# One core, attention beside an expert layer: who copies the expert result out of its bank, and how the first operands come in

## The chip, the cores and the metric

The kernel runs on one core of one Trainium2 chip. The metric is the device time of one execution in microseconds (us); lower is better. A core has five engines that run their own instruction lists and wait for each other by semaphores: TensorE (PE: matmuls, PEld: its weight loads), VectorE (DVE), ScalarE (ACT), GpSimd (POOL) and SyncE (SP), which here only issues transfers. Transfers are carried by 16 DMA engines.

## The reference

For each of 8 batches of 512 tokens with 128 features the kernel computes x + attention(xn) + experts(xn), where xn is x after a layer norm without scale.

```python
qkv = xn @ w_in.T + b_in                      # 16 heads of 8
scores = einsum('bhqd,bhkd->bhqk', q * scale, k) + causal_bias
out = (softmax(scores) @ v) @ w_out.T + b_out
# experts: 8 routed of width 176, the best 2 of each token, and a shared one of width 352
combine = top2(softmax(xn @ gate_w.T)), normalised, * 2.5
y = sum_e combine[:, e] * ((silu(xn @ w_gate[e]) * (xn @ w_up[e])) @ w_down[e])
result = x + out + y + shared_expert(xn)
```

All of it is in float32; the kernel keeps that precision by splitting numbers into parts: the attention's q and k into three bfloat16 parts, the experts' activations and weights into a high and a low part.

## The kernel before

**Stages.** The program of every engine alternates between two stages. In `experts_and_maxima(b, ...)` TensorE runs the gate, up and down matmuls of the 14 expert tiles of batch b, summing the result turned (features by tokens) in the bank `bank_y`; between the tiles it computes the plain scores of batch b in 18 units (`scores`, line 613), of which VectorE takes the row maxima (line 1273). In `attend(i, ...)` TensorE computes the scores of batch i once more, transposed, in 18 units (`scores_t`, line 678, with the mask at 691), into two pairs of banks in turn; ScalarE takes the exponential of each unit (line 974); TensorE weighs v with them (`weigh_v`, line 707). Unit n of `scores_t` waits until ScalarE is done with unit n - 2. The order is written out by hand in each engine's list, and an engine never overtakes within its own.

**What else stands in `attend`.** The front of the next batch is prepared there: ScalarE takes k (line 887), VectorE takes v, splits k, takes q (line 1170), splits q (lines 1160 to 1166), and then adds the tokens to the expert result (`add_tokens`, line 1326), computes the router's weights and more. SyncE writes the parts of k and q to memory (lines 394 and 400) and, once all six writes have landed and half of the transposed units are done, loads them back spread over the partitions as `q_op` and `k_op` (`operands_in`, line 455): 512 KB each for a half of the heads. Behind them stand the routing weights: one small write (line 406) and 18 loads of `cb` (line 411), for GpSimd, which weighs the routed hidden values (line 1055). TensorE starts the plain scores of the next batch (line 613, unit 0) near the end of `attend`; unit 9 is the first to need the second half of the heads.

**The expert result.** In `attend`, ScalarE copies `bank_y` to `yT` (`take_y`, line 958; the profile calls that memory o_sb) behind its second exponential. TensorE turns it back with four transposes (`transpose_y`, line 662) behind unit 3 of the transposed scores, and VectorE adds the tokens to it.

**The first batch** has lists of its own. VectorE normalises, makes `bq_scaled` (line 1500, it needs the q and k weights' semaphore), the low parts of the shared weights (line 1477), splits x, takes the router's maxima and logits (1194, 1196) and v, computes the router's weights (1216 to 1230), casts three constants to bfloat16 (1470 to 1472), copies `combT` (1237), takes q, splits q and k, and only then multiplies the first hidden tile (line 1249). ScalarE converts the weights' high parts (994), takes the turned x, takes the exponential for the router (892), takes k. SyncE issues the token loads of batches 2 to 7 (`tokens_in`, line 366, three of 512 KB) ahead of the first operands.

## Time and profile before

| what | value |
|---|---|
| median of 3 runs | 555.38 us (553.04 to 557.18) |
| the profiled execution | 554.11 us, of which 552.3 us are the span from first to last instruction |
| mean granted clock of TensorE | 0.994 of full speed |
| busy: TensorE, VectorE, ScalarE, GpSimd | 512.5, 430.5, 330.6, 229.6 us |
| one batch in the middle, from one first q projection to the next | 64.0 to 64.8 us |

The profile is read in this order: the busy shares say which engine can bound the kernel; the chain of waits says through which lines the end was reached; the timeline of one stage says which engine waits for which there. A row of the timeline has the start, the length, the engine, the line, the operation with what it writes and reads, how many such instructions were merged, and in brackets the idle time of that engine before it with what ended it. Matmuls overlap, so the lengths of neighbouring TensorE rows can add up to more than the time between them.

### The profile page before, as it was taken

What the parts mean: (1) busy time and instruction counts of PE and PEld (TensorE: products, weight loads), DVE (VectorE), ACT (ScalarE), POOL (GpSimd) and SP (SyncE); (2) the same over time, 40 slices, a digit from 0 to 9 for tenths busy, and PEclk for the clock granted to TensorE, in tenths of its full rate; (3) what the DMA queues carried; (4) which work ended last, traced back from release to release, by engine and by line L of the source; (5) the groups of instructions that cost most, each with busy time, mean ns of one, the idle gap of its engine ahead of it and who ended that gap; (6) DMA issues with size and microseconds to landing.
All of it is one profiled execution on the core that took longest, in us unless ns stands there. A gap on an engine that the chain in (4) does not pass through costs nothing.

```text
span 552.3 us, 16880 instructions
## 1 busy us (share of the span) xinstructions
PE 512.5 (93%) x6840; PEld 321.2 (58%) x6840; DVE 430.5 (78%) x845; ACT 330.6 (60%) x454; POOL 229.6 (42%) x201
## 2 busy tenths in 40 slices
PE   1589999999999999999999999999999999999995
PEld 1355654676557664576546664576646765467643
DVE  3989988899859968598757968599686978489713
ACT  6322489445873469544894458834696348844593
POOL 2026810587007840379005870078403790058600
PEclk9979999999999999999999999999999999999999
DMA  9887016900367005750169003770068302590000
GB/s 261 219 242 181 2 67 163 259 5 11 117 188 196 2 11 162 207 132 1 68 170 258 16 11 116 192 193 1 11 188 219 94 1 78 149 270 16 11 21 21
DMA packets 46896, 62.55 MB, mean 113 GB/s; under 512 B 6672, under 2 KB 30448, under 8 KB 46832
## 3 DMA queue, kind: packets, MB, share of 16 engines
q1 hardware_dynamic: 44124, 58.34, 38.6%
q10 hardware_dynamic: 2708, 3.24, 1.8%
q8 instruction: 54, 0.88, 0.7%
q14 instruction: 10, 0.08, 0.1%
HBM read 45.18 MB, written 15.34 MB: 110 GB/s over the span
## 4 chain that ended last, share of the span: by engine, by line
PE 70%; DVE 8%; ACT 7%; issue 5%; DMA 5%; POOL 4%; SPq 1%; ACTq 0%; DVEq 0%
PE banks L577 9%; PE banks L579 8%; PE banks L578 8%; PE banks L613 7%; PE banks L593 7%; PE banks L707 7%; ACT probs L974 5%; PE banks L678 5%; PE banks L594 4%; PE banks L595 4%; DVE neg_max L1273 3%; DMA k_op<-k_dram 2%; POOL hid_lo L1063 2%; PE banks L532 2%; DMA wqk_sb<-in_wqkT 1%
## 5 line engine op out<-in xcount | busy, mean ns | idle before, releaser
L1273 DVE TENSOR_REDUCE neg_max<-banks 128x2 f32<-128x1024 f32 (+7 forms) x240 | 177.9, 790 | 30.1 <-PE banks L604 28.8
L1063 POOL TENSOR_TENSOR hid_lo<-probs,hid_hi 128x512 fp32r<-128x512 f32 x85 | 109.5, 1288 | 214.5 <-ACT hid_hi L911 214.2
L974 ACT ACTIVATE probs<-banks 128x1024 f32<-128x1024 f32 x144 | 139.1, 1026 | 16.4 <-PE banks L691 15.2
L1055 POOL TENSOR_TENSOR probs<-probs,cb 128x512 f32<-128x512 f32 x88 | 113.1, 1285 | 76.1 <-ACT probs L904 75.5
L904 ACT ACTIVATE probs<-banks 128x512 f32<-128x512 f32 (+1 forms) x112 | 66.8, 598 | 124.2 <-PE banks L579 123.1
L1249 DVE TENSOR_TENSOR probs<-probs,banks 128x512 f32<-128x512 f32 (+1 forms) x112 | 75.9, 679 | 33.3 <-POOL probs L1055 24.9
L577 PE MATMUL banks<-x_hi,w_hi 128*128 128x512 f32 (+1 forms) x224 | 95.6, 427 | 4.8 <-DVE probs L1249 4.1
L579 PE MATMUL banks<-x_hi,w_lo 128*128 128x512 f32 (+1 forms) x224 | 89.5, 400 | 0.0
L578 PE MATMUL banks<-x_lo,w_hi 128*128 128x512 f32 (+1 forms) x224 | 88.9, 397 | 0.0
L911 ACT ACTIVATE hid_hi<-probs 128x512 fp32r<-128x512 f32 (+1 forms) x96 | 60.3, 628 | 38.4 <-DVE probs L1249 38.4
L707 PE MATMUL banks<-probs,v_op 64*32 64x512 f32 (+7 forms) x2048 | 78.5, 410 | 0.0
L678 PE MATMUL banks<-q_op,k_op 64*64 64x512 bf16 (+7 forms) x1024 | 57.4, 295 | 7.2 <-ACT probs L974 6.4
L613 PE MATMUL banks<-k_op,q_op 64*64 64x448 bf16 (+7 forms) x1024 | 54.6, 293 | 5.7 <-DVE neg_max L1273 2.9
L593 PE MATMUL banks<-hid_hi,wd_hi 128*128 128x512 f32 (+1 forms) x112 | 55.3, 494 | 2.6 <-POOL hid_lo L1063 2.3
L577 PEld LDWEIGHTS banks<-x_hi,w_hi 128*128 128x128 f32 (+1 forms) x224 | 42.2, 188 | 21.1 <-DVE probs L1249 5.0
L678 PEld LDWEIGHTS banks<-q_op,k_op 64*64 64x64 bf16 x1024 | 20.2, 105 | 49.4 <-ACT probs L974 31.9
L579 PEld LDWEIGHTS banks<-x_hi,w_lo 128*128 128x128 f32 (+1 forms) x224 | 42.1, 188 | 10.6
L578 PEld LDWEIGHTS banks<-x_lo,w_hi 128*128 128x128 f32 (+1 forms) x224 | 42.4, 189 | 8.5 <-issue 0.5
L707 PEld LDWEIGHTS banks<-probs,v_op 64*32 64x32 f32 x2048 | 30.6, 106 | 27.0 <-issue 16.9
L613 PEld LDWEIGHTS banks<-k_op,q_op 64*64 64x64 bf16 x1024 | 20.6, 105 | 42.6 <-issue 22.4
L594 PE MATMUL banks<-hid_hi,wd_lo 128*128 128x512 f32 (+1 forms) x112 | 44.6, 399 | 0.0
L595 PE MATMUL banks<-hid_lo,wd_hi 128*128 128x512 f32 (+1 forms) x112 | 44.5, 397 | 0.0
(138 smaller groups left out, 556.7 us busy)
## 6 DMA issues: line engine op xcount, KB each, us to landing
cb<-c_dram SPq DMA_DIRECT2D x31, 256.0 KB, 4.0
q_op<-q_dram SPq DMA_DIRECT2D x15, 512.0 KB, 6.3
k_op<-k_dram SPq DMA_DIRECT2D x15, 512.0 KB, 7.4
cb<-c_dram SPq DMA_DIRECT2D x16, 224.0 KB, 4.7
q_dram<-q_parts SPq DMA_DIRECT2D x8, 384.0 KB, 2.9
k_dram<-k_parts SPq DMA_DIRECT2D x8, 384.0 KB, 2.6
cb<-c_dram SPq DMA_DIRECT2D x16, 192.0 KB, 3.8
cb<-c_dram SPq DMA_DIRECT2D x15, 160.0 KB, 4.0
```

The source lines that it names most:

```text
L577: pe.matmul(bank, w_hi[:, w, cols], x_hi[:, :], start=True, stop=False)
L578: pe.matmul(bank, w_hi[:, w, cols], x_lo[:, :], start=False, stop=False)
L579: pe.matmul(bank, w_lo[:, w, cols], x_hi[:, :], start=False, stop=True).then_inc(ready, 1)
L593: pe.matmul(bank_y[:, :], wd_hi[0:n, tile, :], hi, start=(k == 0), stop=False)
L613: pe.matmul(bank[rows, a, at:at + n], q_op[own, 2 * g + c, HALF * jq:HALF * (jq + 1)], k_op[own, 2 * g + c, 0:n], start=first, stop=False, ...
L678: pe.matmul(ring[half(c), 2 * ((n + 1) % 2) + a, at:at + S - HALF * jk], k_op[half(a), 2 * g + c, HALF * jk:HALF * (jk + 1)], q_op[half(a) ...
L707: mm = pe.matmul(nat[32 * j:32 * j + 32, c, HALF * jk:S], v_op[half(c), jk ^ c, t, j, :], probs[half(c), 2 * home_of(units[x]) + a, at[x]: ...
L974: nc.scalar.activation(probs[:, 2 * home_of(n):2 * home_of(n) + 2, :], ring[:, at:at + 2, :], ACT.Exp).then_inc(exp_done, 1)
L1055: nc.gpsimd.tensor_tensor(sg[k % 3][:, :], sg[k % 3][:, :], cb[:, tiles_of(b)[k], :], ALU.mult).then_inc(weighted, 1)
L1063: nc.gpsimd.tensor_tensor(hid_lo[0:n, k % 3, :], hid[k % 3][0:n, :], hid_hi[0:n, k % 3, :].bitcast(F32), ALU.subtract).then_inc(hid_lo_don ...
L1249: nc.vector.tensor_tensor(hid[k % 3][0:n, :], sg[k % 3][0:n, :], ring[0:n, up_bank(k), :], ALU.mult).then_inc(hid_done, 1)
L1273: return nc.vector.tensor_reduce(out, in_, AX.X, ALU.max, negate=True)
```

## The change

Three things are changed.

1. `take_y` moves from ScalarE (behind its second exponential) to VectorE (between taking q and splitting q), and TensorE's `transpose_y` moves from behind unit 3 to behind unit 5 of the transposed scores.
2. In every later batch the first half of the operands is loaded in two quarters: q and k of the first quarter of the heads (256 KB each, counted by `ops_first`), then q and k of the second quarter (`ops_loaded[0]`). Plain scores unit 0 waits for the first pair alone, unit 4 for the second. The first batch was loaded so already.
3. In the first batch the three casts of constants and the taking of q move from VectorE to ScalarE; `bq_scaled` moves behind the router's logits; the three token loads move behind the loads of the routing weights.

On TensorE, in `attend`, before (from unit 3 on; each unit is rows of `q_op,k_op` and a row of masks; `ident_sb,o_sb` is `transpose_y`, `probs,v_op` a weighing):

```order
L678 MATMUL banks<-q_op,k_op 64x448 x4
L678 MATMUL banks<-q_op,k_op 64x64 x4
L691 MATMUL banks<-ident_half,mask_half 64x2x64 x4
L662 MATMUL banks<-ident_sb,o_sb 128x128 x4
L678 MATMUL banks<-q_op,k_op 64x384 x4
L678 MATMUL banks<-q_op,k_op 64x128 x4
L691 MATMUL banks<-ident_half,mask_half 64x2x64 x4
L707 MATMUL banks<-probs,v_op 32x512 x8
L678 MATMUL banks<-q_op,k_op 64x384 x4
L678 MATMUL banks<-q_op,k_op 64x128 x4
L691 MATMUL banks<-ident_half,mask_half 64x2x64 x4
```

and now:

```order
L679 MATMUL banks<-q_op,k_op 64x448 x4
L679 MATMUL banks<-q_op,k_op 64x64 x4
L692 MATMUL banks<-ident_half,mask_half 64x2x64 x4
L679 MATMUL banks<-q_op,k_op 64x384 x4
L679 MATMUL banks<-q_op,k_op 64x128 x4
L692 MATMUL banks<-ident_half,mask_half 64x2x64 x4
L708 MATMUL banks<-probs,v_op 32x512 x8
L679 MATMUL banks<-q_op,k_op 64x384 x4
L679 MATMUL banks<-q_op,k_op 64x128 x4
L692 MATMUL banks<-ident_half,mask_half 64x2x64 x4
L663 MATMUL banks<-ident_sb,o_sb 128x128 x4
L679 MATMUL banks<-q_op,k_op 64x320 x4
L679 MATMUL banks<-q_op,k_op 64x192 x4
```

The four transposes have moved behind the first weighing and unit 5.

On VectorE, at the same place now (`o_sb<-banks` is the copy of `bank_y`):

```order
L1173 TENSOR_SCALAR qk_f<-banks,bq_scaled 128x512
L1178 COPY o_sb<-banks 128x512
L1163 CAST q_parts<-qk_f 128x512
L1165 TENSOR_TENSOR qk_rest<-qk_f,q_parts 128x512
L1167 CAST q_parts<-qk_rest 128x512
L1169 TENSOR_TENSOR q_parts<-qk_rest,q_parts 128x512
L1333 TENSOR_TENSOR x_sb<-banks,x_sb 128x512
```

Before, the same rows stood there without the copy: it lies ahead of the whole split of q.

At the start of the kernel, on ScalarE now (from the second conversion of weights on):

```order
L989 ACTIVATE w_hi<-probs 128x1408
L1004 ACTIVATE ident_bf<-ident_sb 128x128
L1005 ACTIVATE ident_half<-probs 128x64
L1006 ACTIVATE mask_half<-probs 128x64
L893 ACTIVATE rt<-rt 128x32
L1010 ACTIVATE qk_f<-banks,bq_scaled 128x512
L888 ACTIVATE qk_f<-banks,bqk 128x512
L905 ACT_TABLE_LOAD
L905 ACTIVATE probs<-banks 128x512 x2
```

Before, only the rows of `rt<-rt` and of k (`qk_f<-banks,bqk`) stood between the conversion and the table load: the casts now stand ahead of the router's exponential, and q ahead of k.

The diff:

```diff
--- before.py
+++ after.py
@@ -256,6 +256,7 @@
         slots_set = sem("slots_set")
         slots_written = sem("slots_written")
         const_made = sem("const_made")
+        casts_made = sem("casts_made")
         wd_loaded = [sem(f"wd_loaded{n}") for n in range(2)]
         w_hi_done = sem("w_hi_done")
         shared_lo = sem("shared_lo")
@@ -383,10 +384,6 @@
             for dst, src in ((mask_f[0:HALF, :], causal[0:HALF, 0:HALF]), (mask_f[HALF:P, :], causal[0:HALF, 0:HALF]),
                              (ident_f[0:HALF, :], ident[0:HALF, 0:HALF]), (ident_f[HALF:P, :], ident[0:HALF, 0:HALF])):
                 sp.dma_start(dst, src).then_inc(consts_loaded, 16)
-            tokens_in(1)
-            tokens_in(2)
-            tokens_in(3)
-
 
             def k_parts_out(j):
                 sp.wait_ge(ksplit_step, 4 * j + 4)
@@ -450,11 +447,12 @@
 
                     sp.wait_ge(st_ready, ST_ALL * i + ST_ALL * (n + 1) // 2)
                 apart(sp, sp_passed)
-                own = slice(n * PAIRS // 2, (n + 1) * PAIRS // 2)
-                for op, dram in ((q_op, q_dram), (k_op, k_dram)):
-                    sp.dma_start(op[:, own, :].rearrange("p i n -> p (i n)"),
-                                 dram[:, :, :, own, :].rearrange("t s d i n -> (s d) t (i n)")
-                                 ).then_inc(ops_loaded[n], 16)
+                parts = [(slice(0, PAIRS // 4), ops_first), (slice(PAIRS // 4, PAIRS // 2), ops_loaded[0])]
+                for own, loaded in (parts if n == 0 else [(slice(PAIRS // 2, PAIRS), ops_loaded[1])]):
+                    for op, dram in ((q_op, q_dram), (k_op, k_dram)):
+                        sp.dma_start(op[:, own, :].rearrange("p i n -> p (i n)"),
+                                     dram[:, :, :, own, :].rearrange("t s d i n -> (s d) t (i n)")
+                                     ).then_inc(loaded, 16)
 
             def store(i):
                 sp.wait_ge(summed, i + 1)
@@ -488,6 +486,8 @@
             weights_around(1)
             operands_in(0, None, 1)
             weights_around(2)
+            for n in range(1, 4):
+                tokens_in(n)
             sp.dma_start(bo_bc[:, :], b_o.partition_broadcast(P)).then_inc(out_weights, 16)
             for j in range(4):
                 for c in range(2):
@@ -623,11 +623,12 @@
                     pe.wait_ge(ops_first, OP_LOADS * 16)
                 elif i is None and n == OWN_UNITS:
                     pe.wait_ge(ops_loaded[0], OP_LOADS * 16)
-                elif n in (0, NAT_ALL // 2):
-
+                elif n == 0:
+                    pe.wait_ge(ops_first, OP_LOADS * 16 * b + OP_LOADS * 16)
+                elif n in (OWN_UNITS, NAT_ALL // 2):
                     pe.wait_ge(ops_loaded[n // (NAT_ALL // 2)], OP_LOADS * 16 * b + OP_LOADS * 16)
                 if i is None and n == 0:
-                    pe.wait_ge(const_made, 4)
+                    pe.wait_ge(casts_made, 3)
                     pe.wait_ge(q_done, 1)
                     pe.wait_ge(k_done, 1)
                 elif i is None and n == 1:
@@ -830,7 +831,7 @@
                     scores_t(i, n)
                     if n == 2 and front:
                         project_q(i + 1)
-                    if n == 3:
+                    if n == 5:
                         transpose_y(i)
                     if n == TURN_COMB_AT and front:
                         transpose_comb(i + 1)
@@ -953,10 +954,6 @@
                     if 1 <= k < NT - LATE_HIGH:
                         high_hidden(b, k - 1)
 
-            def take_y(i):
-                act.wait_ge(down_done, NT * i + NT)
-                nc.scalar.activation(yT[:, :], bank_y[:, :], ACT.Copy).then_inc(y_taken, 1)
-
             def attend(i, front):
                 if front:
                     take_k(i + 1)
@@ -973,8 +970,6 @@
                     at = 2 * ((n + 1) % 2)
                     nc.scalar.activation(probs[:, 2 * home_of(n):2 * home_of(n) + 2, :], ring[:, at:at + 2, :], ACT.Exp
                                          ).then_inc(exp_done, 1)
-                    if n == 1:
-                        take_y(i)
                     if front and n == 1:
                         exp_router(i + 1)
 
@@ -1005,7 +1000,15 @@
             high_routed(0)
             take_xT(0)
             high_routed(1)
+            act.wait_ge(consts_loaded, 16 * 5)
+            nc.scalar.activation(ident_bf[:, :], ident_sb[:, :], ACT.Copy).then_inc(casts_made, 1)
+            nc.scalar.activation(ident_half[:, :], ident_f[:, :], ACT.Copy).then_inc(casts_made, 1)
+            nc.scalar.activation(mask_half[:, :], mask_f[:, :], ACT.Copy).then_inc(casts_made, 1)
             exp_router(0)
+            act.wait_ge(const_made, 1)
+            act.wait_ge(q_ready, 1)
+            nc.scalar.activation(qk_f[:, 0, :], nat[:, 0, :], ACT.Identity, bias=bq_scaled[:, 0:1], scale=QSCALE
+                                 ).then_inc(q_done, 1)
             take_k(0)
             experts(0, None, True)
             attend(0, True)
@@ -1169,6 +1172,10 @@
                 dve.wait_ge(q_ready, j + 1)
                 nc.vector.tensor_scalar(qk_f[:, 0, :], nat[:, 0, :], QSCALE, bq_scaled[:, 0:1], ALU.mult, ALU.add
                                         ).then_inc(q_done, 1)
+
+            def take_y(i):
+                dve.wait_ge(down_done, NT * i + NT)
+                nc.vector.tensor_copy(yT[:, :], bank_y[:, :]).then_inc(y_taken, 1)
 
             def split_q(j):
                 split_qk(j, 0, q_done, q_parts, qsplit_step, q_written)
@@ -1448,6 +1455,8 @@
                     take_v(i + 1, vl)
                     split_k(i + 1)
                     take_q(i + 1)
+                take_y(i)
+                if front:
                     split_q(i + 1)
                 add_tokens(i)
                 if front:
@@ -1465,12 +1474,6 @@
                 else:
                     add_numbers(i - 1)
 
-            def constants():
-                dve.wait_ge(consts_loaded, 16 * 5)
-                nc.vector.tensor_copy(ident_bf[:, :], ident_sb[:, :]).then_inc(const_made, 1)
-                nc.vector.tensor_copy(ident_half[:, :], ident_f[:, :]).then_inc(const_made, 1)
-                nc.vector.tensor_copy(mask_half[:, :], mask_f[:, :]).then_inc(const_made, 1)
-
             def low_shared():
                 dve.wait_ge(w_hi_done, 1)
                 own = slice(SPLIT, FT)
@@ -1496,18 +1499,16 @@
             mean_and_variance(0)
             reciprocal_root(0)
             normalise(0)
-            dve.wait_ge(qk_weights, 16 * 2)
-            nc.vector.tensor_scalar(bq_scaled[:, :], bqk[:, 0:1], QSCALE, None, ALU.mult).then_inc(const_made, 1)
             low_shared()
             split_x(0, nat[:, 0, :])
             router_logits(0, vl_first)
+            dve.wait_ge(qk_weights, 16 * 2)
+            nc.vector.tensor_scalar(bq_scaled[:, :], bqk[:, 0:1], QSCALE, None, ALU.mult).then_inc(const_made, 1)
             dve.wait_ge(bv_loaded, 16 * 2)
             take_v(0, vl_first)
             dve.wait_ge(consts_loaded, 16 * 5)
             router_weights(0)
-            constants()
             take_combT(0)
-            take_q(0)
             split_q(0)
             split_k(0)
             first_experts_and_maxima()
```

## Rows read from the trace of the kernel before

**Rows 1.** The page: shares of the chain of waits that ended last.

```profile
PE 70%; DVE 8%; ACT 7%; issue 5%; DMA 5%; POOL 4%; SPq 1%; ACTq 0%; DVEq 0%
```

**Rows 2.** Timeline, third attention stage, ScalarE and TensorE.

```profile
206.16 0.59 ACT L958 ACTIVATE o_sb<-banks 128x512 f32<-128x512 f32 x1
...
207.99 2.01 ACT L974 ACTIVATE probs<-banks 128x1024 f32<-128x1024 f32 x2 [0.21 <-PE banks L691]
...
210.39 8.68 ACT L974 ACTIVATE probs<-banks 128x1024 f32<-128x1024 f32 x9 [0.39 <-PE banks L691]
...
211.57 0.41 PE L678 MATMUL banks<-q_op,k_op 64*64 64x320 bf16 x8
...
212.38 0.41 PE L678 MATMUL banks<-q_op,k_op 64*64 64x256 bf16 x8 [0.34 <-ACT probs L974]
```

**Rows 3.** Timeline, last attention stage, ScalarE.

```profile
529.98 12.61 ACT L974 ACTIVATE probs<-banks 128x1024 f32<-128x1024 f32 x13 [0.15 <-PE banks L691]
```

**Rows 4.** The stretch of rows 2 and what follows: VectorE, transfers, first plain scores, GpSimd.

```profile
207.57 0.75 DVE L1170 TENSOR_SCALAR qk_f<-banks,bq_scaled 128x512 f32<-128x512 f32 x1
...
216.77 1.11 SPq L455 DMA_DIRECT2D k_op<-k_dram  x1
...
218.10 0.28 DVE L1237 COPY combT<-banks 32x128 f32<-32x128 f32 x1 [1.42 <-PE banks L550]
...
223.77 0.41 PE L613 MATMUL banks<-k_op,q_op 64*64 64x512 bf16 x4 [0.85 <-DMA k_op<-k_dram]
...
223.83 2.21 SPq L411 DMA_DIRECT2D cb<-c_dram  x5
...
231.26 1.28 POOL L1055 TENSOR_TENSOR probs<-probs,cb 128x512 f32<-128x512 f32 x1 [0.20 <-ACT probs L904]
```

**Rows 5.** Timeline, the last boundary between two batches.

```profile
474.39 0.59 SPq L455 DMA_DIRECT2D k_op<-k_dram  x1
...
480.78 0.41 PE L613 MATMUL banks<-k_op,q_op 64*64 64x512 bf16 x4 [0.51 <-DMA k_op<-k_dram]
```

**Rows 6.** The page, DMA issues: KB each, median us from issue to landing.

```profile
cb<-c_dram SPq DMA_DIRECT2D x31, 256.0 KB, 4.0
```

**Rows 7.** Line 440, 256 KB operand loads of the first batch: microseconds from issue.

```profile
DMA to landing us min/median/max: 4.0/4.6/5.7
```

**Rows 8.** Line 455, 512 KB operand loads of all batches: microseconds from issue.

```profile
DMA to landing us min/median/max: 5.1/6.6/9.7
```

**Rows 9.** Timeline, start of the kernel.

```profile
10.01 1.24 SPq L385 DMA_DIRECT2D probs<-in_ident  x2
...
13.50 0.16 DVE L1500 TENSOR_SCALAR bq_scaled<-bqk 128x1 f32<-128x1 f32 x1 [2.93 <-DMA wqk_sb<-in_wqkT]
...
16.67 0.23 ACT L892 ACTIVATE rt<-rt 128x32 f32<-128x32 f32 x1 [2.97 <-DVE rt L1196]
...
17.15 0.18 DVE L1216 TENSOR_REDUCE rt_s<-rt 128x4 f32<-128x32 f32 x1
...
20.95 0.19 DVE L1230 SCALAR_TENSOR_TENSOR comb<-rt,rt_s 128x32 f32<-128x32 f32 x1
...
22.73 0.43 DVE L1160 CAST q_parts<-qk_f 128x512 bf16<-128x512 f32 x1
...
27.97 0.74 PE L577 MATMUL banks<-x_hi,w_hi 128*96 128x512 f32 x1 [4.11 <-DVE probs L1249]
...
35.06 1.42 DVE L1264 TENSOR_TENSOR hid_lo<-probs,hid_hi 96x512 fp32r<-96x512 f32 x1 [1.69 <-ACT hid_hi L911]
```

**Rows 10.** DMA issues from 0 to 45 us: size, median microseconds to landing.

```profile
probs<-in_ident SPq DMA_DIRECT2D x2, 16.0 KB, 5.4
```

**Rows 11.** Busy us by stretch (PE, PEld, DVE, ACT, POOL); granted clock, DMA share, GB/s.

```profile
28.00:32.00 4.00, 4.00 (x9) 2.30 (x9) 4.00 (x4) 1.69 (x3) 0.00 (x0) 0.50 0.99 309
36.00:56.00 20.00, 17.56 (x195) 10.64 (x196) 20.00 (x30) 5.51 (x9) 11.36 (x11) 1.00 0.80 198
```

**Rows 12.** Timeline, end of the first attention stage, VectorE.

```profile
94.65 1.23 DVE L1273 TENSOR_REDUCE neg_max<-banks 128x2 f32<-128x1024 f32 x1 [0.68 <-PE banks L604]
```

## The prediction

> **What bounds the kernel now.** I read the chain of waits first: 70% of it is TensorE, and DVE, ACT and DMA have 8, 7 and 5% [rows 1]. So a saving counts only where TensorE waits, or where another engine carries the chain. Three such places lie in the change: the attention stage, the boundary between two batches, and the start. I read the timeline of each.
>
> In the attention stage the exponentials run in trains without a gap: nine in 8.68 us, or 0.964 us each [rows 2]. TensorE waits for them later in the train: 0.34 us at unit 8 [rows 2]. Before unit 7 its rows of that stage show no such wait, and it is ScalarE that sits idle, 0.21 us before exponential 3 and 0.39 before exponential 5 [rows 2]. At the boundary TensorE stood 0.85 us for `k_op` in one batch and 0.51 in another [rows 4, 5]; in the five others it did not wait measurably. In the first batch VectorE is full: 4.00 of 4.00 us and 20.00 of 20.00 us [rows 11], so what leaves its list there moves the end.
>
> **Term 1, the copy of `bank_y` and its turn.** ScalarE loses 0.59 us between exponentials 1 and 2 in each of the 8 attention stages [rows 2]. That is 4.7 us of work, but the path is TensorE's: the four transposes are not removed, they go from behind unit 3 to behind unit 5, both ahead of unit 7. With no waits TensorE reaches unit 7 at 211.57 as before and has its masks done some 0.5 us later (0.41 by its row and a tenth for the masks), at 212.1. ScalarE gets there sooner: exponential 3 still starts at 207.99, since it waits for unit 3 behind the projection of q; but unit 5 is now done before exponential 4 ends, so the 0.39 us gap goes, and exponential 6 ends at 207.99 + 4 x 0.964 = 211.85. Exponential 7 starts at the later of the two, 212.1; before it started at 210.39 + 2 x 0.964 = 212.32. Gain: 0.23 us. From there the train sets the pace and carries the 0.23 to the end. It is 7 x 0.23 = 1.6. In the last stage, without the projection, 0.15 us of idle time stands before the long train [rows 3], and a similar sum gives 0.1. **Term 1 = -1.7 us.** Bounds: nothing, if TensorE's unit 7 really ends at 212.3; and 8 x 0.39 = 3.1, the whole gap.
>
> VectorE gets the copy: 0.75 us by its nearest row, the taking of q from such a bank [rows 4]. It waits for nothing new, since the last down matmul lies ahead of the projection of q on TensorE, for which VectorE has just waited. It ends near 209.1, and the turn is now due only at about 209.7. Behind it stand the split of q, `add_tokens` and the router's weights, all 0.75 us later. VectorE then sits idle 1.42 us before `combT` [rows 4]: that covers the 0.75, and `split_x` and what follows come when they did. In the first attention stage there is no such gap, because statistics fill it; there the idle time before the first maxima is 0.68 [rows 12], which leaves 0.1 us. Only the parts of q reach SyncE later, which is term 2.
>
> **Term 2, the quarters.** TensorE was ready at 223.77 - 0.85 = 222.92 and at 480.78 - 0.51 = 480.27. The issue of k's first load moves from 216.77 to 217.5 and from 474.39 to 475.1 by the late split. With half the bytes ahead of it, it should land as line 440's loads of the same shape do: 4.0, 4.6, 5.7 us [rows 7] against 5.1, 6.6, 9.7 for the halves [rows 8]. With 4.6 that is 222.1 and 479.7: the waits go, less perhaps 0.1. **Term 2 = -1.3 us** (bounds: -1.4, and -0.5 at 5.7, where k comes at 223.2 and 480.8 and TensorE still waits 0.3 and 0.5). The second pair is first needed at unit 4, far later. SyncE issues two transfers more, some 0.6 us each [rows 5], ahead of the routing weights. These were issued from 223.83, land in 4.0 us at the median [rows 6] and are first used at 231.26 [rows 4]: issued 0.75 + 1.2 later, the first is there at 229.8, 1.5 us early.
>
> A rule speaks against this: the Trainium skill, DMA: Bandwidth & Descriptors, Anatomy of one DMA, gives each transfer a fixed part of about 2.0 us and the rest at 436 GB/s, and says under Bandwidth to batch to 1 MiB or more. By its figures (an estimate) 256 KB less on each of two loads saves only 1.2 us of landing, and the term would be -0.9.
>
> **Term 3, the start.** VectorE's list loses the casts and the taking of q. The wait of 2.93 us for the q and k weights goes too [rows 9], but not to the end: the router's chain is then held by ScalarE, where the casts stand ahead of the exponential. The last of the constants is issued at about 10.6 and lands 5.4 us later [rows 9, 10], at 16.0; three casts at 0.23 to 0.3 each (the exponential of 32 columns took 0.23) end at 16.8, the exponential at 17.05. So VectorE's chain starts at 17.1, against 17.15 before, and ends at 21.1 as before. From there to the first cast of q it took 22.73 - 21.14 = 1.59; now there is only the turn of the router's weights and the copy of `combT`, 0.28 for the copy [rows 4] and about as much for the turn, 0.55. **Term 3 = -1.0 us**, carried by the full VectorE through the first batch. Bounds: 0 (constants land a microsecond later) and -2.2 (they land by 15: the chain starts at once behind v). ScalarE's q and k are ready by about 19.2, long before VectorE asks. The token loads are needed only for the statistics in the first attention stage, and their move costs nothing; it takes nothing off the constants either, which are issued ahead of them.
>
> Sum: -1.7 - 1.3 - 1.0 = -4.0 us on the profiled execution, 554.11 to 550.1. That execution lies 1.27 us under the median of 555.38, so I forecast **551.4 us**, -0.7%. About 1% (5.5 us) is what a measurement of this kernel can tell from no change; this lies within it.
>
> **The rivals.**
> *Less comes through* (chance 0.19). TensorE's unit 7 ends where exponential 7 began before, and the quarters take 5.7 us. For it: the margin in term 1 is 0.23 us and rests on a modelled end of a matmul. Then terms 1 and 2 are 0 and -0.5: 555.38 - 1.5 = 553.9.
>
> *TensorE's clock holds at the start* (0.17). TensorE stood idle 4.11 us until 27.97 [rows 9] and was granted 0.50 of full speed, its 1.2 GHz level, from 28 to 32 [rows 11]; its slow matmuls are why VectorE then sat 1.69 us [rows 9]. Now it waits about 3.7 us there. If the clock holds, the 1.69 go as well: -5.7, 549.7; with the other terms near their better ends 548. Against it: 3.7 is nearly 4.11, and a new pause of some 1.5 us, for the router's weights, comes just before. The Trainium skill, TensorE: Matmul & The Clock Gate, The HAM clock gate, calls the window over which activity is judged free-running, so that the moment of the change varies between executions; that allows either outcome.
>
> *The quarters are slower than the halves* (0.06): four loads of shorter rows, with q's parts 0.75 us late. At each of 7 boundaries TensorE then waits 0.75 us more plus what the landing loses, less some 0.3 of slack. The other terms bring 2.7, or 0.4 per boundary, so the kernel turns slower when k's quarter lands later than about 6.6 us after its issue. At 8.0, between the halves' median and their 9.7, it is 7 x (0.75 + 1.4 - 0.3) = 13 more: 555.4 + 13 - 2.7 = 566. Against it: the four loads of this size landed in 5.7 at most.
>
> *The change does nothing that shows* (0.06): constants land late, the gap at unit 7 stays, waits move into other batches: 555.4.
>
> **How the numbers follow.** The forecast's own case has 0.52, with 549.5 to 553 as its range. The range for 8 in 10 takes in *less comes through* and most of the clock's case: 547.5 to 555.5. Faster by over 1% means below 549.8: most of the clock's case, and 0.12 of the forecast's own with terms at their better ends: 0.27. Slower by over 1%: 0.06. Within: 0.67.
>
> **What would show it.** Term 1: in an attention stage ScalarE's train has no gap before exponential 5, one of some 0.2 before exponential 7, and the stage is 0.2 us shorter; no gap at 7 means more. Term 2: no wait for `k_op` at line 613's first unit, landing near 4.6. Term 3: the router's sum still starts near 17.1, held by ScalarE; the first split of q at 21.7, the first gate matmul after the pause at 26.9. The forecast fails if that pause ends without a fall of the clock, if TensorE waits for `yT` behind unit 5, or if VectorE is no longer idle before `combT` in the middle batches.

## The result, and the profile after

The changed kernel took **557.23 us** (median of 22 runs, 554.99 to 559.68) against 555.24 for the kernel before (22 runs, 553.02 to 557.35): ratio 1.0029, 95% interval 1.0016 to 1.0042. It is slower by 0.3%, 1.6 to 2.0 us. The forecast of 551.4 had the wrong sign, and the time lies 1.7 us outside its range. It is within 1%, the case that had 0.67; the interval is much narrower than the 1% that the prediction took as what a measurement can tell.

The profiled execution took 558.2 us with a span of 556.4, 4.1 more than that of before (552.3). It lies 1 us above its median as the other lay 1 us below its own, so the traces show about twice the typical difference. The first question is where the 4.1 arise. The projection of q (TensorE, line 532) begins each attention stage's part with q; I took its time in all seven, and the distance from it to the first plain score of the next batch.

TensorE, before, third attention stage (each row: start, length in us, engine, line, operation):

```profile
206.41 1.13 PE L532 MATMUL banks<-xnT,wqk_sb 128*128 128x512 f32 x2
...
207.86 0.66 PE L662 MATMUL banks<-ident_sb,o_sb 128*128 128x128 f32 x4
...
208.85 1.09 PE L707 MATMUL banks<-probs,v_op 64*32 64x512 f32 x16
```

The same stretch after, TensorE and ScalarE:

```profile
207.90 1.12 PE L532 MATMUL banks<-xnT,wqk_sb 128*128 128x512 f32 x2
...
209.25 0.39 PE L679 MATMUL banks<-q_op,k_op 64*64 64x384 bf16 x8
...
210.07 1.09 PE L708 MATMUL banks<-probs,v_op 64*32 64x512 f32 x16 [0.37 <-DVE qk_f L1173]
...
211.49 0.66 PE L663 MATMUL banks<-ident_sb,o_sb 128*128 128x128 f32 x4
...
213.50 0.41 PE L679 MATMUL banks<-q_op,k_op 64*64 64x320 bf16 x8
...
214.10 3.77 ACT L971 ACTIVATE probs<-banks 128x1024 f32<-128x1024 f32 x4 [0.48 <-PE banks L692]
...
224.73 0.41 PE L613 MATMUL banks<-k_op,q_op 64*64 64x512 bf16 x4
```

Counted from the projection of q, the turn came at 1.45 us and the first weighing (`weigh_v`) at 2.44. Now the weighing comes at 2.17, and TensorE has waited 0.37 us there **for VectorE's taking of q**; the turn follows, in time that was full. Unit 7 is reached at 5.60 instead of 5.16 (211.57 in [rows 2]), ScalarE's exponential 7 starts at 6.20 instead of 5.91 (the latter worked out from the train in [rows 2]), and the first plain score stands at 16.83. Before it was 16.45 in the five stages without a wait for operands. The seven stages now take 17.08, 16.84, four times 16.83 to 16.84, and 16.68.

The view of waits (engine, line, tile, waited for; us in total, times, longest), first after:

```profile
PEld banks L679 <- ACT probs L971: 28.5, 50, 1.0
ACT probs L971 <- PE banks L692: 21.4, 57, 0.9
PE banks L613 <- DMA k_op<-k_dram: 4.7, 3, 2.9
PE banks L708 <- DVE qk_f L1173: 3.0, 7, 0.8
```

And before, where the last of these has no row at all:

```profile
PEld banks L678 <- ACT probs L974: 31.9, 65, 0.8
ACT probs L974 <- PE banks L691: 15.2, 38, 0.9
PE banks L613 <- DMA k_op<-k_dram: 2.4, 3, 1.0
```

ScalarE waits 6.2 us more for scores, although it has 4.7 us less to do: the idle time grew on the engine that was relieved.

The last stage has no projection of q, and it too is longer, by 0.42 us from its first transposed score to the end of the kernel (29.16 against 28.74). There TensorE waits for ScalarE at unit 4, before and after:

```profile
528.04 0.41 PE L678 MATMUL banks<-q_op,k_op 64*64 64x384 bf16 x8 [0.26 <-ACT probs L974]
...
531.57 0.41 PE L679 MATMUL banks<-q_op,k_op 64*64 64x384 bf16 x8 [0.82 <-ACT probs L971]
```

The boundary that answers to [rows 5], and the second half of the operands behind it:

```profile
477.13 0.55 SPq L453 DMA_DIRECT2D q_op<-q_dram  x1
477.72 1.29 SPq L453 DMA_DIRECT2D k_op<-k_dram  x1
479.07 0.59 SPq L453 DMA_DIRECT2D q_op<-q_dram  x1
479.70 0.60 SPq L453 DMA_DIRECT2D k_op<-k_dram  x1
480.35 0.67 SPq L403 DMA_DIRECT2D c_dram<-combT  x1
...
483.20 0.41 PE L613 MATMUL banks<-k_op,q_op 64*64 64x512 bf16 x4
...
485.00 8.67 SPq L408 DMA_DIRECT2D cb<-c_dram  x18
...
494.47 0.71 SPq L453 DMA_DIRECT2D k_op<-k_dram  x1
...
503.54 0.41 PE L613 MATMUL banks<-k_op,q_op 64*64 64x512 bf16 x4 [1.09 <-DMA k_op<-k_dram]
```

The first unit waits no more, here or at any boundary. But the routing weights leave SyncE 4.35 us later than before (480.65), where the kernel as a whole is 2.7 late; the second half, issued behind them, is waited for at unit 9: 1.09 us here and 0.70 at 244.69. Before, no unit 9 waited. In these two batches the second half's k left SyncE 11.27 and 11.54 us behind the first plain score; before, this distance was 9.3 to 10.4 us in every batch.

The start, answering to [rows 9]:

```profile
15.93 0.31 ACT L1004 ACTIVATE ident_bf<-ident_sb 128x128 bf16<-128x128 f32 x1 [1.91 <-DMA probs<-in_ident]
...
16.75 0.18 DVE L1223 TENSOR_REDUCE rt_s<-rt 128x4 f32<-128x32 f32 x1 [0.66 <-ACT rt L893]
...
21.41 0.41 DVE L1163 CAST q_parts<-qk_f 128x512 bf16<-128x512 f32 x1
...
26.62 0.74 PE L577 MATMUL banks<-x_hi,w_hi 128*96 128x512 f32 x1 [4.08 <-DVE probs L1256]
...
29.95 0.43 PE L594 MATMUL banks<-hid_hi,wd_lo 128*128 128x512 f32 x1
...
31.92 0.55 SPq L437 DMA_DIRECT2D k_op<-k_dram  x1
...
36.14 0.41 PE L613 MATMUL banks<-k_op,q_op 64*64 64x512 bf16 x4 [2.89 <-DMA k_op<-k_dram]
```

Busy us by stretch, with granted clock, DMA share and GB/s last, after:

```profile
28.00:32.00 4.00, 3.73 (x12) 2.20 (x11) 4.00 (x5) 1.22 (x3) 0.00 (x0) 0.75 0.81 282
36.00:40.00 4.00, 3.86 (x27) 2.34 (x28) 2.00 (x4) 1.21 (x2) 1.41 (x2) 0.61 1.05 279
```

The router's sum starts 0.4 us earlier (16.75 against 17.15); the first cast of q and the end of TensorE's pause come 1.3 us earlier. The first plain score does not: 36.14 against 36.30. TensorE stood 2.89 us ahead of it, its granted clock, full again since 30, fell once more (0.61 in the mean from 36 to 40, before 1.00), and VectorE is 2.00 us busy from 36 to 40, where before it was 4.00. The next batch's q is projected at 78.08, 0.48 later than before (77.60). The last section shows that this 0.48 compares two courses of the clock, so it can't be put down to the change.

**The account of the 4.1 us:** start +0.48; seven stages +0.63, 5 x 0.38, +0.24, or +2.8; last stage +0.42; the waits at unit 0 -0.85 and -0.51; those at unit 9 +0.70 and +1.09. The sum is 4.1.

### The profile page after: what moved, and what is told of

Same layout as the page of the kernel before. It is cut to its first block, busy times and chain, and to the rows that moved or that the text cites. A ratio compares the mean times of both kernels' runs of the same rounds, so it can differ in the third digit from the quotient of the medians.

```text
span 556.4 us, 16902 instructions
## 1 busy us (share of the span) xinstructions
PE 510.8 (92%) x6840; PEld 320.6 (58%) x6840; DVE 434.1 (78%) x849; ACT 329.4 (59%) x450; POOL 229.6 (41%) x201
## 4 chain that ended last, share of the span: by engine, by line
PE 62%; DMA 9%; DVE 8%; SPq 6%; ACT 5%; issue 5%; POOL 3%; ACTq 0%; DVEq 0%
PE banks L577 7%; PE banks L708 7%; PE banks L579 7%; PE banks L593 6%; PE banks L578 6%; PE banks L613 6%; PE banks L679 5%; DMA k_op<-k_dram 4%; PE banks L594 4%; PE banks L595 4%; ACT probs L971 4%; SPq L408 3%; DVE neg_max L1280 2%; POOL hid_lo L1066 2%; DMA q_dram<-q_parts 2%
## 5 line engine op out<-in xcount | busy, mean ns | idle before, releaser
L679 PE MATMUL banks<-q_op,k_op 64*64 64x512 bf16 (+7 forms) x1024 | 56.2, 294 | 8.6 <-ACT probs L971 7.7
L708 PEld LDWEIGHTS banks<-probs,v_op 64*32 64x32 f32 x2048 | 30.8, 105 | 30.2 <-issue 20.8
```

The source lines that it names most:

```text
L679: pe.matmul(ring[half(c), 2 * ((n + 1) % 2) + a, at:at + S - HALF * jk], k_op[half(a), 2 * g + c, HALF * jk:HALF * (jk + 1)], q_op[half(a) ...
L708: mm = pe.matmul(nat[32 * j:32 * j + 32, c, HALF * jk:S], v_op[half(c), jk ^ c, t, j, :], probs[half(c), 2 * home_of(units[x]) + a, at[x]: ...
```

## The experiments

All are edits of the kernel before unless said. Each ratio is to runs of the kernel before, taken beside it on the same chip. The medians of the kernel before were 554.5, 554.33, 555.08 and 555.25 in the four series, so ratios are compared, not medians; a difference of ratios is turned into us at 555 us.

### One part at a time

**Part 1** (copy on VectorE and turn behind unit 5):

```diff
-                    if n == 1:
-                        take_y(i)
...
-                    if n == 3:
+                    if n == 5:
                         transpose_y(i)
...
+                take_y(i)
+                if front:
                     split_q(i + 1)
```

> Part 1 of the change alone: VectorE copies bank_y, the turn stands behind unit 5; operands and first batch as before. Theory P (the place of the turn): behind unit 3 the four transposes filled time in which TensorE would have waited anyway, for VectorE's q in the seven stages with a next batch and for ScalarE in the last; behind unit 5 they lie on the path. By the changed kernel's trace that is 0.6 us in the first stage, 0.4 in each of six and 0.45 in the last: +3.3 us, and TensorE waits for qk_f before the first weighing. Rival V (VectorE's copy makes q's parts late and so the operands): the waits for k_op grow, the stage up to the last unit is as long as before. Rival F (the forecast): -1.7 us.

Measured: 560.78, ratio 1.0115 (1.0084 to 1.0147). The loss is here, and larger than expected. **The turn alone** (second hunk only):

> Only the turn is moved behind unit 5; ScalarE keeps the copy behind its second exponential, VectorE's list is that of before. Theory P: the same wait for qk_f before the first weighing and the same loss as with the copy moved, +2.5 to +4 us, since ScalarE's 0.59 us were not on the path. Rival V: no loss, since VectorE's list is untouched: -1 to 0 us.

Measured: 557.51, ratio 1.0053 (1.0031 to 1.0076). Moving four transposes past two units costs 2.9 us by itself; its undisturbed stages take 17.05 and 16.83 to 16.84, as in the whole change, with seven waits for `qk_f`. They do so although ScalarE still makes the copy here.

**The quarters** (`operands_in`, `ops_first`, the waits of `scores`):

```diff
-                own = slice(n * PAIRS // 2, (n + 1) * PAIRS // 2)
-                for op, dram in ((q_op, q_dram), (k_op, k_dram)):
+                parts = [(slice(0, PAIRS // 4), ops_first), (slice(PAIRS // 4, PAIRS // 2), ops_loaded[0])]
+                for own, loaded in (parts if n == 0 else [(slice(PAIRS // 2, PAIRS), ops_loaded[1])]):
...
```

> Part 2 alone: quarters in later batches. Theory Q (the quarters help at unit 0, but the two more issues and the later write of the routing weights push the loads of the second half back by 1 to 2 us): no wait for k_op at unit 0, a wait of 0 to 1 us at unit 9 in some batches; -1.4 to +0.5 us. Forecast of the prediction: -1.3 us and no wait at unit 9.

Measured: 554.29, ratio 1.0003 (0.9982 to 1.0024). **The first batch** (casts, taking of q and the token loads as in the change):

```diff
-            constants()
             take_combT(0)
-            take_q(0)
```

> Part 3 alone: casts and q on ScalarE, token loads later. Theory K (k's parts reach memory no sooner than before, so the first scores cannot start sooner and TensorE waits 2.9 us, after which its clock falls once more): +0.5 us; the first gate matmul after the pause at 26.6, the first score matmul still at about 36.1. Forecast of the prediction: -1.0 us.

Measured: 554.7, ratio 0.9994 (0.9974 to 1.0013). Neither part shows alone, but the intervals are wide: -1.0 to +1.3 us for the quarters, which just leaves out the forecast -1.3, and -1.4 to +0.7 for the first batch, which takes in the forecast -1.0.

### Why the turn's place costs

Three of its four transposes are left out (so a quarter of y is turned), behind unit 3 and behind unit 5.

```diff
-                for q in range(QT):
+                for q in range(1):
```

> The kernel before, with one of the four transposes of y's turn left out of three (a quarter of y is turned, the rest of the output is not), behind unit 3 as before. Theory P (behind unit 3 the turn fills time in which TensorE would wait for ScalarE's exponentials and for q anyway): three transposes of 0.16 us less in each of 8 stages, 3.7 us in all, bring nothing; time within 0.5 us of before, the wait of TensorE for ScalarE at unit 4 (0.34 us) grows by about what the turn loses and the first weighing waits some 0.2 us for VectorE's taking of q. Rival R (every instruction of TensorE in the transposed scores is on the path): 3.7 us faster.

> The same shortened turn (one of four transposes) behind unit 5, ScalarE copying y. Theory P (behind unit 5 the turn is on the path, the gap that it leaves at unit 3 is one that TensorE waits out anyway): 3.0 to 3.7 us below the full turn behind unit 5 (557.5), so 553.8 to 554.5, within 0.5 us of before, although the wait for q before the first weighing stays at 7 times. Rival Q (the wait for q before the first weighing is what costs, wherever the turn is): as the full turn behind unit 5, 557 to 557.5.

Measured: 554.07, ratio 0.9992 (0.9975 to 1.0010), and 556.27, ratio 1.0023 (1.0004 to 1.0043). Behind unit 3 the removal of half of the turn's time is worth nothing that shows in the medians (the interval reaches to 1.4 us). Behind unit 5 it is worth 1.7 us of the 2.9 (1.0053 against 1.0023), less than the 3.0 to 3.7 expected, and the place still costs. Their traces say why. TensorE, short turn behind unit 3:

```profile
207.97 1.13 PE L532 MATMUL banks<-xnT,wqk_sb 128*128 128x512 f32 x2
...
209.42 0.33 PE L662 MATMUL banks<-ident_sb,o_sb 128*128 128x128 f32 x1
...
210.14 1.09 PE L707 MATMUL banks<-probs,v_op 64*32 64x512 f32 x16
...
212.96 0.41 PE L678 MATMUL banks<-q_op,k_op 64*64 64x320 bf16 x8
```

And behind unit 5:

```profile
207.45 1.12 PE L532 MATMUL banks<-xnT,wqk_sb 128*128 128x512 f32 x2
...
209.63 1.09 PE L707 MATMUL banks<-probs,v_op 64*32 64x512 f32 x16 [0.28 <-DVE qk_f L1170]
...
211.05 0.33 PE L662 MATMUL banks<-ident_sb,o_sb 128*128 128x128 f32 x1
...
212.73 0.41 PE L678 MATMUL banks<-q_op,k_op 64*64 64x320 bf16 x8
```

The first weighing starts 2.17 and 2.18 us after q's projection, and in no trace sooner: it writes the bank from which VectorE takes q, and its list entry waits for that (`q_done`). What stands behind unit 3 fills that time; what stands behind unit 5 is added to it. In microseconds from q's projection, third stage for unit 7, an undisturbed middle stage for the end:

| | weighing | unit 7 | first plain score |
|---|---|---|---|
| short turn behind 3 | 2.17 | 4.99 | 16.23 |
| before, turn behind 3 | 2.44 | 5.16 | 16.45 |
| short turn behind 5 | 2.18 | 5.28 | 16.51 |
| turn behind 5 (the whole change) | 2.17 | 5.60 | 16.83 |

So the full turn behind unit 3 delays the weighing by only 0.27 us, and behind unit 5 all of it is on the path. Each row's end moves with its unit 7, within 0.1 us. Two expectations were off in size. The three transposes left out are 0.33 us a stage (0.66 against 0.33 in the rows), not three times 0.16; and behind unit 3 they are not free, since each stage is 0.22 us shorter (16.23 against 16.45), 1.5 us in seven stages, somewhat more than the medians show.

**q projected one unit earlier**, turn behind unit 5, to take the wait away:

```diff
-                    scores_t(i, n)
                     if n == 2 and front:
                         project_q(i + 1)
+                    scores_t(i, n)
```

> The full turn behind unit 5 (ScalarE copies), with the projection of the next batch's q before unit 2 of transposed scores instead of behind it. Theory P2 (the first weighing can't start sooner than 2.17 us after the projection of q, when VectorE has taken it from the bank; behind unit 3 the turn used most of that time, behind unit 5 it is 0.28 us of idle and the turn's 0.65 us comes on top): the wait for q before the first weighing is gone in all 7, and q's projection to the first plain score, corrected for the unit that now stands between, shrinks by about 0.28 us a stage; 1.5 to 2 us below the turn behind unit 5 alone, 555.5 to 556. Rival Q2 (TensorE then waits the same time for ScalarE's exponentials, whose unit 2 comes later): no gain, 557.5.

Measured: 557.84, ratio 1.0047 (1.0030 to 1.0064), against 1.0053 with the turn moved alone: no gain that shows. The wait for q is gone, and another has come at unit 4, for ScalarE's exponential 2, since unit 2 now stands behind the projection:

```profile
209.02 1.02 PE L532 MATMUL banks<-xnT,wqk_sb 128*128 128x512 f32 x2
...
211.57 0.41 PE L678 MATMUL banks<-q_op,k_op 64*64 64x384 bf16 x8 [0.85 <-ACT probs L974]
```

The slack at this place has two owners, q's bank and the exponentials. The last stage, which has no q, says the same: without the turn behind unit 3 the wait for ScalarE at unit 4 grew from 0.26 to 0.82 us. This reordering did not remove the slack. Whether a bank of its own for q would was not tried.

### Do the parts depend on each other?

**Parts 1 and 2** (their diffs above together), and **parts 2 and 3**, the whole change with part 1 undone (diff against the whole change):

```diff
-                    if n == 5:
+                    if n == 3:
                         transpose_y(i)
...
+                    if n == 1:
+                        take_y(i)
...
-                take_y(i)
-                if front:
                     split_q(i + 1)
```

> Part 1 and the quarters, with the first batch as before. Theory H (VectorE's copy of y delays q's parts by 0.75 us, so that operands are late at unit 0 in some stages; the quarters land earlier and hide that): time 557 to 557.8, as the whole change, 3 us below part 1 alone; no wait for operands at unit 0 in any stage. Rival X (part 1 alone at 560.8 is a loss of its own that the quarters do not touch): 560 or more.

> The whole change without part 1 (quarters and the reordered first batch; ScalarE copies y, turned behind unit 3). Theory P (part 1 is the loss, and the others are worth nothing that shows): 554 to 555, within 0.5 us of before and 2 to 3 us below the whole change. Rival I (the parts hurt each other: the later start makes the quarters' second half wait at unit 9): 556 or more.

Measured: 557.73, ratio 1.0061 (1.0039 to 1.0084), and **553.39, ratio 0.9976 (0.9961 to 0.9992)**. With the quarters, part 1 costs what the turn alone costs, and its trace has no wait at unit 0. The trace of part 1 alone had three (0.47, 0.34, 0.64 us); in sum 1.45 us against the 1.36 of before, so this trace does not account for the whole difference of 3 us. It can't: at 557.95 it was the fastest of six executions, 2.8 below their median. Late q parts are a guess at the cause, not a shown one. Without part 1 the rest of the change gains 1.3 us (0.4 to 2.2), more than expected.

### The start

**k first**: part 3 alone, the first load of q's operand also held until k is written.

```diff
-                        if g == 0 and op is k_op:
+                        if g == 0 and op is q_op:
```

> Part 3 alone (casts on ScalarE, its taking of q, tokens after the routing weights), with the first load of q's operand also waiting until k's parts are written. Theory K (at the start q's operand load is under way while k's parts are written, and delays them: written 5.9 us after issue against 4.5): k is written by about 30.5, first plain scores at 34.5 to 35 instead of 36.1, granted clock full again by 36 or not lost, 0.5 to 1.5 us faster than part 3 alone, so about 553.5. Rival L (the landing time is the DMA's latency whatever else is under way, and the later load of q takes its place): first plain scores at 36 or later, time 554.5 to 556.

Measured: 556.01, ratio 1.0028 (1.0011 to 1.0045). The loads that wait for k left at 32.08, no earlier: the load of q is not what delays k. **Routing weights late**: part 3, with the first group's 512 KB loaded by SyncE behind the first operands.

```diff
-                act.wait_ge(comb_written, 16)
-                for t, p0, n, e in SEGMENTS[0]:
-                    act.dma_start(cb[p0:p0 + n, t, :], c_dram[e, :].partition_broadcast(n)).then_inc(cb_loaded[0], 16)
...
+            weights_around(0)
             weights_around(1)
```

> Part 3 alone, with the first group of routing weights (512 KB in three loads, which ScalarE issues at 24.7 us beside the writing of k's parts) loaded by SP behind the first operands instead. Theory K2 (what makes the last of k's parts take 6.0 us from issue to landing is what else the DMA engines carry from 24 to 31 us, the routing weights' 512 KB first): k is written by 30.5 to 31 instead of 31.9, first plain scores at 34.7 to 35.2, TensorE's pause shorter by about 1 us; the whole is 0.3 to 1 us below part 3 alone, less what GpSimd loses because its weights land later (it used them at 32.6). Rival L2 (the landing of k does not depend on them): first plain scores at 36.0 or later, and the whole no faster than part 3 alone, 554.7 or more.

Measured: 557.44, ratio 1.0035 (1.0020 to 1.0051). The mechanism was right and the price wrong:

```profile
29.54 0.55 SPq L437 DMA_DIRECT2D k_op<-k_dram  x1
...
33.91 0.41 PE L613 MATMUL banks<-k_op,q_op 64*64 64x512 bf16 x4 [0.44 <-DMA k_op<-k_dram]
...
38.30 2.48 POOL L1060 TENSOR_TENSOR probs<-probs,cb 128x512 f32<-128x512 f32 x2 [33.74 <-DMA cb<-c_dram]
...
41.53 0.64 PE L613 MATMUL banks<-k_op,q_op 64*64 64x320 bf16 x8 [3.88 <-DVE neg_max L1278]
```

Against part 3 alone, k is written 2.4 us earlier (29.5 against 32.0) and the scores come 2.4 us earlier (33.91 against 36.32). But GpSimd, which multiplied its first tile at 32.63 there, waits until 38.30; VectorE waits for GpSimd, and TensorE then stands 3.88 us for VectorE's maxima, with its clock at 0.50 from 40.2 to 47.0. So I split the group on top of parts 2 and 3: tile 0 as before, tile 1 later.

```diff
-CB_GROUPS = [range(0, 2), range(2, 5), range(5, ROUTED)]
+CB_GROUPS = [range(0, 1), range(1, 2), range(2, 5), range(5, ROUTED)]
...
             weights_around(1)
-            operands_in(0, None, 1)
             weights_around(2)
+            operands_in(0, None, 1)
+            weights_around(3)
```

> Parts 2 and 3 without part 1 (553.4), and the first group of routing weights in two: tile 0 (256 KB, one load) by ScalarE as before, tile 1 (256 KB, two loads) by SP behind the first operands, each with its own semaphore. Theory K3 (the first group's bytes delay k's parts, and GpSimd's need of tile 0 is what made the later load costly): k written by 30.5 to 31, first plain scores at 34.8 to 35.3, GpSimd at 32.6 to 33 for its first tile and not later than 37.5 for its second; 0.3 to 1 us below parts 2 and 3, about 552.7. Rival (GpSimd's second tile is then the late one, as it was the first before): 554 to 556, with GpSimd's wait for the weights in the trace.

> Parts 2 and 3 without part 1 once more. If their gain is real, 553 to 554 and again some 0.2% below the kernel before; if it was chance, 554.5 to 555.5.

Measured: **552.59, ratio 0.9947 (0.9928 to 0.9966)**, and 553.24, ratio 0.9963 (0.9946 to 0.9980). The gain of parts 2 and 3 came again. The split version has the lowest median of all, as expected, though its interval overlaps that of parts 2 and 3. Its start:

```profile
30.18 0.55 SPq L437 DMA_DIRECT2D k_op<-k_dram  x1
...
32.93 1.27 POOL L1065 TENSOR_TENSOR probs<-probs,cb 128x512 f32<-128x512 f32 x1 [28.38 <-ACT probs L906]
...
34.20 0.41 PE L614 MATMUL banks<-k_op,q_op 64*64 64x512 bf16 x4 [0.66 <-DMA k_op<-k_dram]
...
37.88 1.26 POOL L1065 TENSOR_TENSOR probs<-probs,cb 128x512 f32<-128x512 f32 x1 [3.68 <-DMA cb<-c_dram]
```

The next batch's q is projected at 75.88 (parts 2 and 3: 76.60 and 76.86; before: 77.60). This instant varies with the course of the clock, which the last section describes: kernels with the start of before showed 77.30 to 81.31. The four traces just named have the same course. Firmer are the landing of k, at 31.90 to 32.05 in all five traces with part 3 and the whole group beside it, and the medians.

### The second quarter later

The quarters alone, with the second quarter issued behind the first routing weights:

```diff
                     weights_around(m)
+                    if m == 0:
+                        second_quarter_in()
...
```

> Quarters alone, with the second quarter's two loads issued behind the first group of routing weights instead of straight behind the first quarter's. Theory S (the quarters push back the routing weights and with them the second half, whose landing makes TensorE wait at unit 9 in two or three stages; what is won at unit 0 is lost there): waits at unit 0 stay away, the routing weights return to their old time after the operands, waits at unit 9 still possible as the second half is issued as late; 0.3 to 1.0 us below the quarters alone, 553.3 to 554. Rival N (where operands are loaded in time anyway, the order of the loads changes nothing that shows): within 0.3 us of the quarters alone, 554 to 554.6.

Measured: 555.44, ratio 1.0010 (0.9989 to 1.0031): nothing won.

## Why the prediction was wrong

**Term 1 (-1.7) was the failed step; it measured +2.9 with the turn alone, and +3.2 in the whole change's trace (2.8 and 0.42).** The whole change (1.0029) against parts 2 and 3 (0.9976 and 0.9963) gives +2.9 and +3.7 for the same step. The sentence that failed is "With no waits TensorE reaches unit 7 at 211.57 as before": I moved the turn between two places ahead of unit 7 and took the sum of TensorE's work there for the time. The first weighing between the two places writes q's bank, and doesn't start before VectorE has q out of it, 2.17 us after the projection. The trace of before shows that limit only as an absence: the turn made TensorE 0.27 us later than it, so no wait was recorded. Unit 7 came 0.44 us late; the rest of my chain then held with its sign turned: exponential 7 starts 0.29 later instead of 0.23 earlier, and the train carries it to the end. In the last stage, forecast at -0.1, the same place is held by ScalarE alone (0.82 us at unit 4), and it cost 0.42. The gap before exponential 5 shrank from 0.39 to 0.20 us, and one of 0.48 opened before exponential 7. The copy on VectorE (0.68 us in the trace, forecast 0.75) did no harm that shows once the quarters were there, as argued. ScalarE's freed 4.7 us were worth nothing that shows: an undisturbed stage takes 16.83 us with the copy on either engine.

**Terms 2 and 3 together were about right.** They forecast -2.3 us; parts 2 and 3 without part 1 measured -1.3 (-2.2 to -0.4) and -2.1 (-3.0 to -1.1).

**Term 2 (-1.3) was right where it looked and incomplete.** The two waits at unit 0 went, 1.36 us in the trace, and the first quarter's k landed 4.4 to 5.0 us after its issue (forecast 4.6; the halves' k before: 6.3 to 7.0). I costed the later routing weights against their own user, GpSimd, but not the operands' second half, which stands behind them in the same queue: 1.79 us of waits at unit 9. Alone, the quarters measured +0.2 us (-1.0 to +1.3). The figures of the Trainium skill that I set against them (DMA: Bandwidth & Descriptors, Anatomy of one DMA) stand there for transfers that GpSimd issues; these are SyncE's. By my estimate from them two loads would land 1.2 us sooner; in the trace k's first load alone landed 1.3 to 2.5 us sooner. So the measurement differs from that estimate, and what ate the term was the place in the queue: the second half's k took 9.0 us from issue to landing at the last boundary, hardly more than the 8.6 before, but left later.

**Term 3 (-1.0) was right to 26.6 us; behind it the forecast had the wrong gate.** ScalarE held the router's chain (16.75, forecast 17.1), the first cast came at 21.41 (21.7), the pause of TensorE ended at 26.62 (26.9). I then let a full VectorE carry the gain through the batch, and never asked what the first scores wait for: k's last part. It was issued 1.35 us earlier (26.00 against 27.35) and written only 0.3 earlier (31.90 against 32.22), since the routing weights' 512 KB move beside it. With all or half of them out of the way it was written at 29.5 or 30.2. Between traces with the same course of the clock, parts 2 and 3 still bring the next projection of q 0.4 to 1.1 us earlier (76.60 and 76.86 against 77.30 to 77.65 in four kernels with the start of before), so most of the gain may have come through by another way than this one; by which is open.

**The rivals.** *Less comes through* named term 1's margin as weak, rightly, but took zero as the worst; a loss was left out without a reason. *TensorE's clock holds* did not happen: the clock fell in the pause of 4.08 us as before. What I had not listed is the second fall, behind the pause of 2.89. That the time fell within 1%, the case with 0.67, is luck: the sum behind it had the wrong sign. The slower side was put on the quarters alone, at 0.06; part 1, the true loser, had none.

## What to carry to other kernels

Before moving an instruction, ask of each neighbour that stays behind which wait it would meet if it came sooner: the moved one may have been filling a slack that no row shows. List the semaphores of the instruction that moves up, and take the distance from each release. And follow a later transfer down its queue to the last one behind it, not only to its own user.

## What I had not expected of the hardware

**One code, two courses of the clock.** Parts 2 and 3 have the same first batch as the whole change, and the traces show nearly the same pause of TensorE (4.08 us, until 26.62 in the whole change, 26.80 and 26.68 in the two executions of parts 2 and 3). Parts 2 and 3, second execution:

```profile
28.00:32.00 4.00, 3.36 (x8) 1.69 (x8) 4.00 (x5) 0.97 (x2) 0.00 (x0) 0.50 0.82 288
32.00:36.00 4.00, 2.89 (x8) 1.95 (x6) 2.31 (x4) 1.11 (x2) 1.28 (x1) 0.70 0.48 116
36.00:40.00 4.00, 3.77 (x45) 2.24 (x49) 3.90 (x6) 1.23 (x2) 1.82 (x2) 1.00 1.07 298
```

Here the granted clock stayed at 0.50 (1.2 GHz) until 34.4; TensorE waited 1.25 us for k and then kept the full 2.4 GHz. In the whole change the clock was back by 30, TensorE was done sooner, waited 2.89 us for the same landing, and worked at 0.50 again from 36.9 to 40.3: next projection of q at 78.08 against 76.60.

All sixteen traces but one follow one of these two courses. In seven the clock stayed at 0.50 as long as before (26.9 to 33.7 there) and did not fall again until the last 3 us of the kernel: before, part 1, the quarters, parts 1 and 2, parts 2 and 3 twice, and the split version. Their next projection of q comes at 75.88 to 77.65. In nine it stayed low only half as long, as in the whole change (26.6 to 30.0), and in eight of these it fell once more between 36.6 and 40.2; the projection comes at 78.08 to 81.46. The ninth is the short turn behind unit 5, without a second fall there, at 78.34. The longer wait for k does not decide it by itself: the first execution of parts 2 and 3 waited 2.51 us and kept its clock,

```profile
36.00:40.00 4.00, 3.60 (x41) 2.20 (x41) 3.65 (x5) 1.23 (x2) 1.56 (x2) 1.00 1.03 283
```

while the short turn behind unit 3 waited 1.98 us and lost it. In these traces an early return of the clock went with a later first batch; why is not shown, nor which course the executions without a trace took. What follows for reading is plain: compare the starts of two traces only if both have the same course. The +0.48 above does not. The Trainium skill (TensorE: Matmul & The Clock Gate, The HAM clock gate) says that the moment of a change is not fixed to the program; the traces agree, with the return at 30.0, 32.1 and 34.4 us behind the same pause.

**A write slowed by its neighbours.** With part 3 in place, the 384 KB of k's last part landed 5.85 to 5.97 us after their issue with 512 KB of routing weights beside them (five traces), 4.3 with 256 KB, and 3.3 with none (one trace each).
